# A three-block decoder on one core: the prologue in another order, the loads of units 2 and 3 held for the first row of maxima, and cross maxima among the visits in steps 6 and 7

## The chip, the cores and the metric

One core of a Trainium2 chip runs the whole program; the other seven are idle. The time is device time in microseconds of one execution, from the runtime's own clock; the profile's span, from the first to the last instruction, is a little shorter. Three runs of the kernel before are shown, and one profiled execution.

## The reference, cut to what matters

Input `x` is 8 sequences of 256 tokens with 128 features. Three residual blocks follow each other, in float32:

```
x = x + attn(layernorm(x))        # 16 heads of 8, chunks of 64 tokens; a chunk sees itself (causal) and the chunk before
x = x + xattn(layernorm(x), ctx)  # 16 heads of 8, 256 queries against 256 context tokens, with a mask and biases
x = x + ffn(layernorm(x))         # int8-rounded activations, ternary weights, 128 -> 512, a width-3 depthwise
                                  # convolution over time, silu, 512 -> 128

attn:  q, k, v = split(x @ w_qkv);  softmax(q k^T / sqrt(8) + mask) v;  @ w_out
xattn: the same with q = x Wq^T + bq, k, v from ctx;  @ Wo^T + bo
```

Each softmax subtracts its row maximum.

## The kernel before, in words

**Units and steps.** There are 16 units: units 0 to 7 are the local attention of sequences 0 to 7, units 8 to 15 the cross attention of the same sequences. The main loop (`for i in range(UNITS): iteration(i)`, one loop per engine, each an in-order instruction stream tied to the others by semaphores) runs one step per unit. Step `i` has 8 beats if it is local and 16 if it is cross (`count_of`). A beat computes one bank of scores for unit `i` on the PE, and ACT takes their exponentials into `probs` (L718). On some beats a *visit* follows (class `Local`, `Cross`, `Cross14`, `Cross15`: the beat after which each piece is issued): `qk_project` of unit `i+5` (L248 to L253), `pv`, the product of probabilities and values (L438, L451), `o_turn` (L463), `max_turn` with `v_project`, `oT_turn` with `x_turn` of unit `i+6`, and `project`, the output projection (L479).

**Maxima.** The scores of a unit are computed twice. The first time, up to two steps ahead, a "max unit" `n` (8 per local unit, 16 per cross unit) goes to bank `3 + n % 3`, and DVE reduces it to negated row maxima (`max_take`, L935). `max_range(i, k)` says which `n` fall in beat `k` of step `i`. Max unit `n` may start only when take `n - 3` is done (`m_max`). For cross units a max unit is two matmuls in one half of the rows of the array; neighbours use different halves, so a pair is issued interleaved (L303). When all maxima of a unit are there, the PE turns them (`max_turn`, L425), ACT copies them (`m_copy`, L736) and a small DMA on ACT's queue (`row`, L817) writes them as one more row of the queries, so that the second computation of the scores comes out with the maximum subtracted. `score_open` waits for that row (`m_row`).

**The split of q and k.** float32 precision in bf16 matmuls is reached by splitting each projection into high, mid and low parts, stacked over 96 rows. For units 0 to 3 ACT takes the high part and DVE the rest; from unit 4 on ACT copies the projection (`raw_copy`) and POOL makes all parts (`high_part`, `rest_part`, `mid_part`, `low_part`). The SP queue stores the parts to DRAM (`store`, 768 KB a unit with its copies) and reads them back in the stacked layout (`load`, 3 DMAs and 768 KB for a local unit) into one of 6 slots of `QK`. Each slot needs zeros once (`query_slot`, a POOL memset, L1302) and a row of ones (`query_row`).

**Prologue.** Before step 0: the first four units are projected and split by all engines together, units 0 and 1 are loaded, the PE computes max units 0 to 7 (unit 0), turns them, then max units 8 to 13 (six of unit 1). In between lie, for unit 4 and 5, `normalise` (DVE), `x_turn`, `qk_project(4)`, and `turn_over(n)`, matmuls whose result nobody reads. POOL ends its prologue with `split(4)`, the zeros of slots 4 and 5, and `mask_r` (L1342), the attention mask as a row, that cross units need. SP runs through `store`, `load` and `query_row` in a fixed order; `load(u)` waits until all parts of `u` have landed in DRAM.

**Step 0 on POOL.** `normalise(6)`, which waits for DVE's statistics of unit 6 (`x_stats`, behind the take of max unit 14); `high_part(5)`; `keep(0, 1)`, the causal select on `probs` (L1241); rest and mid part; `keep(0, 3)`; low part; `keep(0, 5)`, `keep(0, 7)`. `pv(0, 0)`, the PE's last visit of step 0, waits for the first two of these selects (`s_kept`).

## Time and profile before

| | us |
|---|---|
| median of 3 runs (295.54 to 297.85) | 296.94 |
| the profiled execution | 288.12 |
| its span | 286.3 |
| PE busy | 256.6 (90%) |
| DVE busy | 213.2 (74%) |
| ACT busy | 201.3 (70%) |
| POOL busy | 141.5 (49%) |

The rows of the profile give start and duration on a common clock from the span's start. A row with "x8" merges eight like instructions that follow each other; the bracket behind a row is the idle time of that engine before it and what ended it. "Lnnn" is a line of the kernel, often that of a helper. "SPq" and "ACTq" rows are DMA issues: how long the queue's engine was occupied, not when the data landed. PEclk is the granted clock of the tensor engine as a share of 2.4 GHz, so 0.50 is 1.2 GHz.

### The profile page before, as it was taken

How to read it: one execution, taken by the hardware profiler on the slowest of the kernel's cores; microseconds unless marked ns; L12 is line 12 of the kernel's file. 1: busy time of each engine (PE TensorE's matmuls, PEld its weight loads, DVE VectorE, ACT ScalarE, POOL GpSimd, SP SyncE). 2: the span in 40 equal slices, each digit the busy share in tenths (PEclk: the TensorE clock that was granted, in tenths of full speed). 3: DMA queues.
4: the chain of work that ended last, by engine and by line, in shares of the span. 5: the costliest groups of instructions: out<-in, count | busy, mean ns of one | idle time of the engine just before them, and what ended most of it. 6: DMA issues, size and time to landing. Idle time of an engine off the chain costs nothing.

```text
span 286.3 us, 8864 instructions
## 1 busy us (share of the span) xinstructions
PE 256.6 (90%) x3395; PEld 161.1 (56%) x3395; DVE 213.2 (74%) x543; ACT 201.3 (70%) x394; POOL 141.5 (49%) x219
## 2 busy tenths in 40 slices
PE   5778969999999999888989898898879998999992
PEld 1554657888888766554555455445434454555541
DVE  6696845676677678899788898988942468997654
ACT  1443286768878877658788887788879956677752
POOL 6579897675965956748596800000062334331000
PEclk9579799999999999999999999999999999999998
DMA  6587664694687797679646630000000000001001
GB/s 190 144 244 222 171 208 134 191 306 130 192 265 188 158 214 136 167 160 186 146 109 126 162 62 3 1 3 3 0 1 3 2 1 0 21 18 29 21 19 47
DMA packets 34435, 31.38 MB, mean 110 GB/s; under 512 B 2725, under 2 KB 30248, under 8 KB 34265
## 3 DMA queue, kind: packets, MB, share of 16 engines
q1 hardware_dynamic: 33680, 30.38, 41.7%
q8 instruction: 27, 0.44, 0.7%
q10 hardware_dynamic: 712, 0.44, 0.5%
q14 instruction: 16, 0.12, 0.1%
HBM read 16.78 MB, written 13.63 MB: 106 GB/s over the span
## 4 chain that ended last, share of the span: by engine, by line
PE 63%; DVE 11%; ACT 7%; issue 6%; POOL 5%; DMA 3%; SPq 2%; ACTq 2%; DVEq 0%; POOLq 0%
PE ps L507 11%; PE ps L438 10%; PE ps L451 6%; DVE negm L935 5%; PE ps L311 5%; PE ps L303 4%; PE ps L368 3%; PE ps L463 3%; DMA stack_parts<-low 3%; ACT probs L718 3%; PE ps L292 3%; PE ps L479 2%; ACTq L817 2%; PE ps L266 2%; PE ps L248 2%
## 5 line engine op out<-in xcount | busy, mean ns | idle before, releaser
L935 DVE TENSOR_REDUCE negm<-ps 128x2 bf16<-128x512 f32 (+1 forms) x192 | 123.0, 691 | 35.1 <-PE ps L331 12.5
L718 ACT ACTIVATE probs<-ps 128x512 f32<-128x512 f32 x192 | 103.9, 601 | 17.8 <-PE ps L368 8.4
L507 PE MATMUL ps<-tapw,xqT 128*128 128x512 f32 x96 | 45.3, 604 | 0.0
L303 PE MATMUL ps<-QK 49*128 49x256 bf16 x256 | 36.2, 272 | 3.4 <-DVE negm L935 3.3
L311 PE MATMUL ps<-QK 50*128 50x256 bf16 x256 | 35.2, 272 | 3.4 <-ACT probs L718 3.3
L438 PE MATMUL ps<-probs,V 128*32 128x256 f32 x512 | 34.1, 385 | 4.5 <-ACT V L706 4.5
L1186 POOL TENSOR_TENSOR ve<-mv,eps 128x2 f32<-128x2 f32 x8 | 1.6, 195 | 55.1 <-DVE mv L972 55.1
L311 PEld LDWEIGHTS ps<-QK 50*128 50x128 bf16 x256 | 17.5, 94 | 19.0 <-ACT probs L718 14.7
L507 PEld LDWEIGHTS ps<-tapw,xqT 128*128 128x128 f32 x96 | 16.8, 190 | 15.4 <-issue 15.4
L368 PE MATMUL ps<-QK 98*128 98x128 bf16 x256 | 23.8, 219 | 0.5
L1241 POOL TENSOR_SCALAR_AFFINE_SELECT probs<-probs 128x512 f32<-128x512 f32 x32 | 21.1, 661 | 6.0 <-ACT probs L718 5.9
L438 PEld LDWEIGHTS ps<-probs,V 128*32 128x32 f32 x512 | 13.5, 109 | 17.2 <-ACT V L706 6.2
L779 ACT ACTIVATE high<-probs,unround 128x512 bf16<-128x512 f32 x15 | 10.8, 722 | 15.3 <-DVE probs L1017 15.3
L303 PEld LDWEIGHTS ps<-QK 49*128 49x128 bf16 x256 | 16.6, 94 | 8.2 <-DVE negm L935 5.2
L368 PEld LDWEIGHTS ps<-QK 98*128 98x128 bf16 x256 | 17.3, 97 | 4.7 <-issue 1.5
L451 PE MATMUL ps<-probs,V 128*32 128x64 f32 x1024 | 17.9, 221 | 2.0 <-POOL probs L1241 1.9
L722 ACT CAST ps<-tri_k 128x512 f32<-128x512 bf16 x30 | 17.7, 590 | 0.9
L1229 POOL TENSOR_TENSOR low<-raw,mid 128x512 bf16<-128x512 f32 x15 | 17.4, 1158 | 1.8 <-DMA stack_parts<-low 1.3
L451 PEld LDWEIGHTS ps<-probs,V 128*32 128x32 f32 x1024 | 15.2, 110 | 4.2 <-issue 3.3
L1002 DVE TENSOR_REDUCE hm<-probs 128x1 f32<-128x512 f32 x16 | 10.9, 682 | 8.2 <-ACT probs L761 8.2
L1167 POOL TENSOR_TENSOR ve<-mv,eps 128x2 f32<-128x2 f32 x16 | 3.1, 195 | 25.6 <-DVE mv L895 25.4
L745 ACT COPY oxT<-ps 128x256 f32<-128x256 f32 (+1 forms) x23 | 10.4, 453 | 5.3 <-PE ps L240 4.5
(138 smaller groups left out, 500.2 us busy)
## 6 DMA issues: line engine op xcount, KB each, us to landing
QK<-stack_parts SPq DMA_DIRECT2D x24, 384.0 KB
stack_parts<-high SPq DMA_DIRECT2D x32, 192.0 KB, 4.4
stack_parts<-mid SPq DMA_DIRECT2D x32, 128.0 KB, 3.7
QK<-stack_parts SPq DMA_DIRECT2D x16, 192.0 KB
stack_parts<-low SPq DMA_DIRECT2D x16, 128.0 KB, 4.2
CT<-in_ctx_t_dram SPq DMA_DIRECT2D x1, 1024.0 KB, 7.9
out_dram<-probs SPq DMA_DIRECT2D x16, 64.0 KB, 1.6
tapw<-in_taps_dram SPq DMA_DIRECT2D x1, 768.0 KB, 6.8
```

The costliest lines, as they stand in the source:

```text
L303: last = nc.tensor.matmul(bank(3 + n % 3)[:, t * S:(t + 1) * S], QK[r, s, 0, pr, t * P:(t + 1) * P], QK[r, s, 2, pr, :], start=(t == 0), s ...
L311: last = nc.tensor.matmul(bank((before(i) + k) % 3)[:, kt * S:(kt + 1) * S], QK[r, s, 2, pr, kt * P:(kt + 1) * P], QK[r, s, 0, pr, :], sta ...
L368: last = nc.tensor.matmul(o[:, x * P:(x + 1) * P].rearrange("p (j q) -> p j q", j=2), KT[r, s, pr, WINDOWS[c]:WINDOWS[c] + P], QT[r, s, :, ...
L438: last = nc.tensor.matmul(o[32 * r:32 * r + 32, half * S:(half + 1) * S], V[:, i % 2, PAIRS * kt + 4 * half + r, 2 * m:2 * m + 2, :], prob ...
L451: last = nc.tensor.matmul(o[32 * r:32 * r + 32, st * S + c * W:st * S + (c + 1) * W], V[:, i % 2, PAIRS * V_AT[c] + 4 * st + r, 2 * m:2 * ...
L507: last = nc.tensor.matmul(bank(UP[u % 3]), xqT[:, b % 2, t * P + k:t * P + k + P], tapw[:, k, :], start=False, stop=(k == 2), skip_group_c ...
L718: nc.scalar.activation(probs[:, k, :], bank(n % 3), ACT.Exp, scale=SCALE).then_inc(s_exp, 1)
L722: nc.scalar.copy(bank(n % 3).rearrange("p (h q) -> p h q", q=W), tri_k[:, min(c, 1), :].unsqueeze(1).to_broadcast([P, 8, W])).then_inc(s_s ...
L935: nc.vector.tensor_reduce(dst, src, AX.X, ALU.max, negate=True).then_inc(m_max, 1)
L1002: nc.vector.tensor_reduce(hm[:, p, 0:1], hid[:, u % 3, :], AX.X, ALU.max, apply_absolute_value=True).then_inc(h_steps, 1)
L1229: nc.gpsimd.tensor_tensor(half_of(low, u), raw[:, :, u % 2 * S:(u % 2 + 1) * S], half_of(mid, u), ALU.subtract).then_inc(low_done, 1)
L1241: nc.gpsimd.affine_select(out=kept, in_=kept, compare_op=ALU.is_ge, fill=0.0, base=W if k >= 2 else 0, pattern=[[0, 8], [1, W]], channel_m ...
```

## The change

The change has two halves. In the prologue: PE's order (`x_turn(4)`, `x_turn(5)`, `qk_project(4)` now come after `max_turn(0)`, in other banks; ten instead of four filler matmuls ahead of max unit 0), ACT's order with it, DVE's (`normalise(4)` behind the rests of units 2 and 3, `normalise(5)` behind take 7), POOL's (`query_slot(2)` sooner; `query_slot(5)` now in step 0 behind `normalise(6)`; `mask_r` now at the end of step 1) and SP's (`store(1, 2)` ahead of `load(0)`, `store(3, 0)` ahead of `load(1)`, and `load(2)`, `load(3)` behind a new wait for the first row of maxima). In steps 6 and 7 (`B - 2`, `B - 1`): on odd beats the max units are issued after the first part of the visit instead of right behind the scores, and step 6 has two max units a beat until its 14 are out.

```diff
--- before.py
+++ after.py
@@ -70,6 +70,8 @@
     def upto(n):
         if i == 0:
             return (0, 1, 2, 2, 2, 3, 4, 5, 6)[n]
+        if i == B - 2:
+            return min(total, 2 * n)
         return min(total, n if total <= beats else -(-total * n // beats))
 
     return range(first + upto(k), first + upto(k + 1))
@@ -403,11 +405,18 @@
                         cross_beat(i, k)
                         return
                     scores(i, k)
-                    if late_pair(i, k):
+                    if late_pair(i, k) or spread(i, k):
                         return
                     if k > 0 and late_pair(i, k - 1):
                         max_late_pair(max_range(i, k - 1)[0])
                         return
+                    maxima(i, k)
+
+                def spread(i, k):
+
+                    return i in (B - 2, B - 1) and k % 2 == 1
+
+                def maxima(i, k):
                     ms = list(max_range(i, k))
                     if len(ms) == 2 and is_cross(max_unit(ms[0])[0]):
                         for m in ms:
@@ -560,6 +569,8 @@
                             pv(i - 1, 1, bank(BX), (0,))
                         if k == at.PV_B and i >= 1:
                             pv(i - 1, 1, bank(BX), (1,) if is_cross(i - 1) else (0, 1))
+                            if spread(i, k):
+                                maxima(i, k)
                         if at is Local and k == at.QK and made is not None:
                             if i >= 2:
                                 pe.wait_ge(y_done, i - 1)
@@ -570,6 +581,8 @@
                             else:
                                 pe.wait_ge(y_done, i - 1)
                             o_turn(i - 1, bank(BY))
+                            if spread(i, k):
+                                maxima(i, k)
                         if k == at.VM and i + 1 < UNITS:
                             if i >= 1:
                                 pe.wait_ge(o_done, i)
@@ -592,12 +605,16 @@
                             if turn is not None:
                                 last = x_turn(turn, bank(BY))
                             last.then_inc(xT_ps, 1)
+                            if spread(i, k):
+                                maxima(i, k)
                         if is_cross(i) and k == at.PV_A:
                             pv(i, 0, bank(BX), (1,))
                         if at is Local and k == at.PV_A:
                             pe.wait_ge(v_sb, i + 2)
                             pe.wait_ge(mT_sb, i + 2)
                             pv(i, 0, bank(BX))
+                            if spread(i, k):
+                                maxima(i, k)
                         if k == at.Y and i >= 1:
                             pe.wait_ge(xT_sb, i + 7)
                             if i == 6:
@@ -625,26 +642,24 @@
                 x_turn(3, bank(7)).then_inc(xT_ps, 1)
                 qk_project(2, bank(3))
                 qk_project(3, bank(4))
-                x_turn(4, bank(6)).then_inc(xT_ps, 1)
                 pe.wait_ge(xT_sb, 4)
-                x_turn(5, bank(7)).then_inc(xT_ps, 1)
-                qk_project(4, bank(5))
-                pe.wait_ge(xT_sb, 6)
-                turn_over(4)
+                turn_over(10)
                 pe.wait_ge(s_pc, PC_ALL)
                 pe.wait_ge(rows_in, 32)
                 for n in range(8):
                     if n < 2:
                         pe.wait_ge(rest_done, 3 + n)
-                    if n == 2:
-                        pe.wait_ge(raw_done, 1)
                     max_unit_mms(n)
-                pe.wait_ge(xT_sb, 5)
                 max_turn(0, bank(BX, BF16))
+                x_turn(4, bank(BY)).then_inc(xT_ps, 1)
+                x_turn(5, bank(1)).then_inc(xT_ps, 1)
+                qk_project(4, bank(0))
                 for n in range(8, max_end(-1)):
                     max_unit_mms(n)
                 pe.wait_ge(s_dc, CONST_ALL)
                 pe.wait_ge(v_sb, 1)
+                pe.wait_ge(xT_sb, 6)
+                pe.wait_ge(raw_done, 1)
                 for i in range(UNITS):
                     if i == 3:
                         pe.wait_ge(wc_in, 16)
@@ -842,14 +857,14 @@
                 ox_copy(2, bank(6), S, 2 * S)
                 ox_copy(3, bank(7), S, 2 * S)
                 high_copy(2, bank(3))
+                high_copy(3, bank(4))
                 v_copy(0, bank(2))
-                ox_copy(4, bank(6), S, 2 * S)
-                high_copy(3, bank(4))
-                ox_copy(5, bank(7), S, 2 * S)
-                raw_copy(4, bank(5))
                 v_slot(1)
                 m_copy(0, bank(BX, BF16))
                 row(0)
+                ox_copy(4, bank(BY), S, 2 * S)
+                ox_copy(5, bank(1), S, 2 * S)
+                raw_copy(4, bank(0))
                 act.wait_ge(s_pc, PC_ALL)
                 for i in range(UNITS):
                     iteration(i)
@@ -1126,13 +1141,14 @@
                 link(nc.vector.memset(bias3[:], 0.0))
                 nc.vector.memset(unround[:], -ROUND)
                 link(nc.vector.memset(onesb[:], 1.0))
-                normalise(4)
-                normalise(5)
                 rest_make(2, bank(3))
                 rest_make(3, bank(4))
+                normalise(4)
                 nc.vector.memset(xqT[:, :, 0:1], 0.0)
                 nc.vector.memset(xqT[:, :, S + 1:S + 2], 0.0).then_inc(padded, 1)
                 for n in range(max_end(-1)):
+                    if n == 8:
+                        normalise(5)
                     max_take(n)
                 for i in range(UNITS):
                     iteration(i)
@@ -1275,6 +1291,8 @@
                     local = not is_cross(i)
                     if i + 6 < UNITS:
                         normalise(i + 6)
+                    if i == 0:
+                        query_slot(5)
                     if i + 5 < UNITS:
                         high_part(i + 5)
                     if local:
@@ -1290,6 +1308,9 @@
                     if local:
                         for k in (5, 7):
                             keep(i, k)
+                    if i == 1:
+                        g.wait_ge(m_in, 16)
+                        nc.gpsimd.tensor_scalar(mask_r[:], mask_i, -MASKED, MASKED, ALU.mult, ALU.add).then_inc(s_mask, 1)
                     if i == 8:
                         quantise(0)
                     if i == 9:
@@ -1327,19 +1348,16 @@
                 g.wait_ge(low_done, 1)
                 mid_part(1)
                 low_part(1)
+                query_slot(2)
                 rstd_part(4, 8)
                 rstd_part(5, 10)
-                query_slot(2)
                 mid_part(2)
                 low_part(2)
                 mid_part(3)
                 low_part(3)
                 query_slot(3)
+                query_slot(4)
                 split(4)
-                query_slot(4)
-                query_slot(5)
-                g.wait_ge(m_in, 16)
-                nc.gpsimd.tensor_scalar(mask_r[:], mask_i, -MASKED, MASKED, ALU.mult, ALU.add).then_inc(s_mask, 1)
                 for i in range(UNITS):
                     iteration(i)
                 ffn_normalise(0)
@@ -1424,18 +1442,19 @@
                 store(0, 2)
                 store(1, 0)
                 store(1, 1)
+                store(1, 2)
                 load(0)
-                store(1, 2)
+                query_row(2)
                 store(2, 0)
+                store(3, 0)
                 load(1)
-                query_row(2)
                 store(2, 1)
-                store(3, 0)
                 store(2, 2)
                 store(3, 1)
-                load(2)
                 store(3, 2)
                 query_row(3)
+                sp.wait_ge(m_row[0], 16)
+                load(2)
                 load(3)
                 query_row(4)
                 stack(4)
```

## Rows read from the trace of the kernel before

**Rows 1.** Windows: busy us (x instructions) of each engine, PEclk, DMA share, GB/s.
```profile
26.00:28.00 2.00, 0.75 (x15) 0.37 (x10) 1.86 (x4) 0.00 (x0) 1.92 (x3) 1.00 0.90 254
...
29.00:32.00 3.00, 3.00 (x24) 2.01 (x22) 2.59 (x4) 0.00 (x0) 1.98 (x2) 0.50 0.45 128
...
41.00:43.00 2.00, 0.31 (x21) 0.34 (x25) 0.58 (x1) 1.51 (x3) 1.93 (x4) 1.00 1.07 313
60.00:100.00 40.00, 39.55 (x855) 32.49 (x852) 28.27 (x61) 32.48 (x66) 30.24 (x45) 1.00 0.72 201
...
114.10:127.50 13.40, 11.12 (x219) 7.54 (x215) 12.11 (x26) 8.03 (x17) 8.10 (x12) 1.00 0.77 180
```

**Rows 2.** The chain that ended last, 31 to 43 us: start us, us, what.
```profile
31.18 3.48 POOL QK L1302 x2
...
34.75 1.89 POOL mask_r L1342
...
41.93 0.63 POOL probs L1241
```

**Rows 3.** Timeline of the PE, prologue: start us, us, engine, line, what.
```profile
16.21 1.06 PE L252 MATMUL ps<-oxT,wp 128*128 128x256 f32 x2
...
18.66 0.60 PE L253 MATMUL ps<-oxT,wp 128*128 128x256 f32 x2
...
20.61 0.60 PE L252 MATMUL ps<-oxT,wp 128*128 128x256 f32 x2
...
21.48 1.03 PE L612 MATMUL ps<-identb 128*128 128x512 bf16 x4
...
22.34 0.38 PE L327 MATMUL ps<-causal,identb 128*128 128x512 bf16 x1
...
28.01 0.27 PE L425 MATMUL ps<-identb,negm 128*16 128x128 bf16 x2 [1.26 <-DVE negm L935]
...
28.21 0.39 PE L327 MATMUL ps<-causal,identb 128*128 128x512 bf16 x1
...
32.65 0.39 PE L361 MATMUL ps<-tri_k,identb 128*128 128x512 bf16 x1
...
42.69 1.10 PE L451 MATMUL ps<-probs,V 128*32 128x64 f32 x64 [1.85 <-POOL probs L1241]
```

**Rows 4.** Timeline of ACT, its queue and DVE in the prologue.
```profile
20.81 0.37 ACT L745 COPY oxT<-ps 128x256 f32<-128x256 f32 x1 [0.44 <-PE ps L240]
...
22.98 4.88 DVE L935 TENSOR_REDUCE negm<-ps 128x4 bf16<-128x512 f32 x8 [1.55 <-PE ps L331]
...
28.32 0.36 ACT L736 COPY mT<-ps 16x256 bf16<-16x256 bf16 x1 [3.24 <-PE ps L425]
...
28.71 0.60 ACTq L817 DMA_DIRECT2D QK<-mT  x1
...
35.10 0.30 DVE L895 BATCH_NORM_AGGREGATE mv<-bnst 128x2 f32<-128x6 f32 x2
```

**Rows 5.** Timeline of the SP queue: issues of load 0 and load 2.
```profile
15.17 1.21 SPq L1395 DMA_DIRECT2D QK<-stack_parts  x2
...
29.96 1.14 SPq L1395 DMA_DIRECT2D QK<-stack_parts  x2
```

**Rows 6.** The chain again: low part of unit 1, issue to landing.
```profile
17.06 3.79 DMA stack_parts<-low
```

**Rows 7.** DMA issues of the page: count, KB each, median us to landing.
```profile
out_dram<-probs SPq DMA_DIRECT2D x16, 64.0 KB, 1.6
```

**Rows 8.** Waits from 100.5 to 127 us: us in total, times, longest.
```profile
PE ps L303 <- DVE negm L935: 2.8, 5, 0.6
```

**Rows 9.** Timeline of DVE at the end of step 7.
```profile
121.60 5.07 DVE L935 TENSOR_REDUCE negm<-ps 128x2 bf16<-128x512 f32 x8
...
127.07 0.42 DVE L951 TENSOR_TENSOR X<-ps,X 128x256 f32<-128x256 f32 x1 [0.40 <-PE ps L479]
```

**Rows 10.** Timeline of the PE at the start of step 8.
```profile
127.55 0.70 PE L248 MATMUL ps<-oxT,wp 128*128 128x256 f32 x2
```

## The prediction

> **What bounds the kernel now.** I read the windows first, to see which stretch has slack. From 60 to 100 us the PE is busy 39.55 of 40 us, so whatever the prologue loses or gains goes straight into the end. Before that there are holes: 0.75 busy of 2 us at 26 to 28, 0.31 of 2 at 41 to 43, and 29 to 32 us run at a granted clock of 0.50, half speed. In step 7, from 114.1 to 127.5, the PE is busy only 11.12 of 13.4 us and DVE 12.11 [rows 1]. Then the chain: the last wait that the prologue ends with is POOL's. Two memsets of query slots (3.48, so 1.74 each, 1.8 with the start), then `mask_r` until 36.64, then step 0's POOL work up to the select `keep(0, 3)`, whose end at 42.56 releases `pv(0, 0)` [rows 2]. The PE starts it at 42.69 after 1.85 us idle [rows 3]. Behind that point no wait of any size is left until step 6, so **the start of pv(0, 0) is the figure that the first half of the change moves**. I work it out in three links.
>
> **Link 1, first row of maxima.** Before, max unit 0 starts at 22.34, behind four fillers begun at 21.48 (0.215 each), its first take at 22.98, eight takes in 4.88, `max_turn(0)` at 28.01. Now the PE is through `qk_project(3)` at 19.26 (18.66 + 0.60) and has ten fillers: 19.26 + 2.15 = 21.4, which is 0.9 sooner [rows 3, 4]. The eight takes keep their pace (DVE sets it: 0.61 each), so `max_turn(0)` comes at 27.1. DVE has `normalise(4)` ahead of them, now beside POOL's splits; it is ready by 22.0, in time for a first take at 22.1. What could hold it up is load 0, now behind `store(1, 2)` and so 0.7 later: issued from 15.9 instead of 15.17 [rows 5]. The trace does not show when it lands. Bounds: the shortest landing on the page is 1.6 us, which gives 19.4; at worst it landed just ahead of its first use at 22.55 and now lands at 23.2, and link 1 gives -0.9 + 1.7 = +0.8 instead. I take the nearest row, the low part issued right behind load 0, which took 3.79 us: the last piece of load 0, done issuing at 17.75, is there by about 21.3 [rows 6, 7]. So -0.9.
>
> **Link 2, from there to the first scores.** Before, `max_turn(0)` is followed at 28.21 by the six max units of unit 1, and the scores of step 0 start at 32.65 [rows 3]. Now two `x_turn` and `qk_project(4)` stand between. `qk_project(4)` needs `ox_copy(4)`, which ACT does after `m_copy` and after issuing `row(0)`: 0.31 until the copy starts, 0.36 copy, 0.60 issue with some 0.1 around it, 0.37 `ox_copy`, 0.14 to the PE, so 1.9 behind the start of `max_turn` [rows 4], which hides both `x_turn`. That is 29.0. The projection takes 1.2 at full clock (twice 0.60) or 2.1 at half (twice 1.06) [rows 3]. The PE again stands still just ahead of `max_turn(0)`, and before it fell to half speed right after such a hole [rows 1]; I take 2.1, so 31.1. The six max units took 4.44, most of it at half speed; at full speed they go at the takes' pace, 6 x 0.61 = 3.7. I take 4.0, some of it slow. First scores at **35.1 instead of 32.65, +2.45**. Bounds: 29.0 + 1.2 + 3.7 = 33.9, +1.25; and 31.1 + 4.44 = 35.5, +2.9.
>
> **Link 3, from the first scores to pv(0, 0).** The PE itself came to it at 40.84 (42.69 less the 1.85), 8.2 behind the first scores, so now by 43.3 at the latest: POOL decides again. POOL's step 0 needs the statistics of unit 6, which are finished at 35.4, that is 2.75 behind the first scores [rows 4], since the take of max unit 14 comes first. Before they waited 1.25 us for `mask_r` to end. Now POOL is through with its prologue early: after `qk_project(4)` a copy of 0.7 and 3.5 of `split(4)`, about 35.5, and starts with the statistics at 35.1 + 2.75 = 37.85. From there to the end of `keep(0, 3)` it was 42.56 - 36.64 = 5.92, and the memset of slot 5, 1.80, now stands in the middle of it: 45.6 [rows 2]. pv(0, 0) starts at 45.7, **+3.0**. Taking `mask_r` and one memset (3.7) out of POOL's prologue gains only the 1.25 that was really waited, and the moved memset costs 1.80 again.
>
> **Costed at nothing.** Holding loads 2 and 3: load 2 was issued at 29.96 in any case [rows 5], since it waited for its low part; the row, issued at 27.8, has landed by then with anything from 1.6 to 2.2 us. Load 3 goes directly behind it and sooner than before; it and everything queued behind on SP (`query_row(4)`, `stack(4)`) is needed only in step 1 and later. Load 2 is needed at max unit 16, 4.7 us into step 0. If the row took 6 us longer, that would be late first. `mask_r` at the end of step 1 lies in the hole that POOL has there before the next statistics, and its reader is unit 8. ACT's `v_slot(1)`, `m_copy(0)` keep their order.
>
> **Steps 6 and 7.** The PE waits for takes 5 times, 0.6 each, 2.8 together, four of them in step 7 [rows 8]: pairs of max units stand with only one beat of scores between, and the second of the pair needs the bank of the take before. In step 6 I find no gain: the singles of beats 3 and 7 become one pair (-0.3), but beats 5 and 6 now adjoin, with a wait of 0.56, and `oT_turn` waits some 0.25 for `norm`, which is now behind two takes. In step 7 the visits go between the pairs and three of four waits go; walking the beats the PE is through 1.26 sooner. But DVE does 12.11 us of work in those 13.4 [rows 1], at 0.634 a take in a row [rows 9], and now becomes the bound: its sixteen takes, norm and statistics put the residual's end at 126.8 instead of 127.49. The next `qk_project` (127.55, right behind that residual [rows 10]) waits for exactly it. So **-0.6**. Bounds: all waits gone and kept, -2.8; the visits delay DVE's first takes more than they save, +0.4.
>
> **Sum.** +3.0 - 0.6 = +2.4. Against the profiled execution: 288.12 + 2.4 = 290.5. The median of the runs lies 8.8 above that execution; I add the same to it: 296.94 + 2.4 = **299.3**.
>
> **The rule that speaks against this.** After the hole at 26 to 28 the granted clock is 0.50 from 29 to 32; after the one at 41 to 43, with even less work in it, it stays 1.00 [rows 1]. The new wait ahead of pv(0, 0), 45.7 - 43.3 = 2.4 or more, is longer than either. The Trainium skill, "TensorE: Matmul & The Clock Gate", Part 1, says that throttled is the default state and activity releases it; by that rule the longer hole is likelier to be followed by half speed. The trace agrees in one of the two holes.
>
> **The rivals.** (a) **Half speed after the longer hole**: three microseconds at 0.50 as at 29 to 32 do 1.5 us less, with load 0 perhaps late besides: 301. For it, the rule and the first hole; against it, the second. Chance 0.22. (b) **The other side, the takes as the whole story**: in steps 6 and 7 spreading removes all 2.8 us of waits because DVE's order absorbs them (it idles 1.3 in step 7 and more in step 6), while link 2 comes at its lower bound. It decides if DVE's residual ends before 126: then +1.8 - 2.8 = -1.0, 295.9. Against it, 12.11 of 13.4. Chance 0.12. (c) **The prologue change does little**: the clock doesn't fall, links 1 and 2 give +1.25 and link 3 adds 0.55, less 0.6: 298.1; or POOL's memset hides in a wait that I have wrong, and it is 297. Chance 0.18. The forecast has 0.48.
>
> **How the numbers follow.** Lower end: prologue +1.8, steps -2.8 and a little of either chance, 296.2. Upper end: +3.4 + 0.4 + 1.5, less the part that needs all three, 301.7. Within 1% is plus or minus 2.97, about what a measurement tells from no change. The forecast lies 0.6 below that border, so a third of its 0.48, most of (a), nothing of (b) and (c) go over: 0.16 + 0.18 = 0.34 slower. Faster by over 1% needs (b) and more: 0.07. Within: 0.59.
>
> **What would show it.** `max_turn(0)` near 27.1; the projection rows of unit 4 (L252, L253) from 29.0; first L361 near 35.1; a memset L1302 between L1178 and L1212 in step 0; L451 first at 45.7 behind POOL's L1241; L303 waits on L935 about 0.6 to 1.2 in sum from step 6 to 7, DVE without idle in step 7. It is wrong if the first scores start before 33.9, if pv(0, 0) isn't released by POOL, or if the PE waits elsewhere for load 2.

## The result and the profile after

The change makes the kernel slower: the ratio of its times to those of the kernel before is **1.0186, 95% interval 1.0147 to 1.0226**. On the 296.94 us that the forecast started from, that is 302.5 us. The ratio compares the executions near each kernel's fastest; single executions of the kernel before spread from 288 to 302 us, those of the changed one from 293 to 300. The plain medians of 20 each are 294.58 and 295.63, too near each other for that spread to call: what is shown is that the changed kernel no longer has executions below 292.7, where the kernel before has six below 291. A second set of runs of the unedited changed kernel gave 1.0287 (1.0229 to 1.0345). The profiled execution of the changed kernel took 295.05 us with a span of 293.3, against 288.12 and 286.3.

The windows of the changed kernel (stretch, its length, busy us and instructions of PE, PE weight load, DVE, ACT, POOL, then PEclk, DMA share, GB/s), which answer to [rows 1]:

```profile
41.00:43.90 2.90, 0.13 (x3) 0.03 (x1) 0.70 (x1) 2.22 (x5) 2.83 (x5) 1.00 0.32 103
45.00:48.40 3.40, 3.40 (x67) 2.28 (x58) 1.20 (x2) 0.80 (x2) 1.11 (x2) 0.65 0.93 283
60.00:65.00 5.00, 4.51 (x93) 3.73 (x94) 3.65 (x8) 2.23 (x4) 2.56 (x4) 0.66 0.36 104
...
121.00:133.70 12.70, 11.19 (x218) 7.54 (x216) 12.00 (x25) 8.54 (x18) 7.99 (x12) 1.00 0.60 128
```

The hole ahead of pv(0, 0) is deeper (0.13 busy of 2.9 us), and two stretches that had a granted clock of 1.00 before now have a mean of 0.65 and 0.66, so that most of each ran at 1.2 GHz: 45 to 48.4 and 60 to 65. The PE's own rows, beside [rows 3]:

```profile
27.48 0.28 PE L434 MATMUL ps<-identb,negm 128*16 128x128 bf16 x2 [1.16 <-DVE negm L950]
...
29.25 0.70 PE L254 MATMUL ps<-oxT,wp 128*128 128x256 f32 x2 [0.82 <-ACT oxT L760]
...
30.22 0.38 PE L329 MATMUL ps<-causal,identb 128*128 128x512 bf16 x1
...
33.37 0.39 PE L363 MATMUL ps<-tri_k,identb 128*128 128x512 bf16 x1
...
43.91 1.93 PE L460 MATMUL ps<-probs,V 128*32 128x64 f32 x64 [2.77 <-POOL probs L1257]
```

`max_turn(0)` is at 27.48 (28.01 before), the projection of unit 4 at 29.25, the six max units begin at 30.22 and the first scores at 33.37 (32.65 before). pv(0, 0) comes at 43.91 instead of 42.69, behind 2.77 us of idle time, and its 64 matmuls take 1.93 us where they took 1.10. What releases it is POOL (lines of the changed kernel: L1228 is the start of `split(4)`, behind 4.53 us of idle time, L1183 the start of `normalise(6)`, L1323 the zeros of slot 5, L1257 `keep`):

```profile
31.07 0.61 POOL L1228 CAST high<-raw 128x512 bf16<-128x512 f32 x1 [4.53 <-ACT raw L712]
...
36.20 0.19 POOL L1183 TENSOR_TENSOR ve<-mv,eps 128x2 f32<-128x2 f32 x1 [1.38 <-DVE mv L910]
...
38.36 1.81 POOL L1323 MEMSET QK<- 128x2048 f32 x1
...
43.10 0.66 POOL L1257 TENSOR_SCALAR_AFFINE_SELECT probs<-probs 128x512 f32<-128x512 f32 x1
```

Then a wait that the kernel before did not have, in the PE's timeline of the changed kernel, and the same thing in its chain of waits:

```profile
60.49 0.62 PE L370 MATMUL ps<-QK 98*128 98x128 bf16 x8 [1.68 <-DMA QK<-mT]
```

```profile
54.15 6.29 DMA QK<-mT
...
80.01 4.54 DMA QK<-mT
```

The row of maxima of unit 2, 8 KB on ACT's queue, was issued at 54.15 and landed 6.29 us later. The row of unit 4, issued at 80.01, took 4.54. Ahead of the row of unit 2 stood SP's transfers (timeline of the SP queue):

```profile
30.24 1.13 SPq L1413 DMA_DIRECT2D QK<-stack_parts  x2
...
48.87 1.37 SPq L1413 DMA_DIRECT2D QK<-stack_parts  x2
...
50.91 0.43 SPq L1463 DMA_DIRECT2D CT<-in_ctx_t_dram  x1
...
52.15 1.33 SPq L1396 DMA_DIRECT2D stack_parts<-high  x2
```

Load 5 (768 KB), the context (1 MB), the cross weights (256 KB) and the high part of unit 6 were issued in the 5.3 us before; the mid and low parts of unit 6 followed the row. In the kernel before load 5 left at 53.77 and the context at 55.59, behind that row's issue at 51.45.

A table by landmarks shows where the rest went. The issue of each unit's row by ACT is a landmark that every trace has.

| | before | changed | difference, running |
|---|---|---|---|
| row of unit 1 | 37.89 | 38.61 | +0.7 |
| row of unit 2 | 51.45 | 54.15 | +2.7 |
| row of unit 3 | 62.77 | 68.80 | +6.0 |
| row of unit 6 | 96.26 | 103.15 | +6.9 |
| row of unit 8 | 121.49 | 127.13 | +5.6 |
| row of unit 10 | 147.59 | 153.01 | +5.4 |
| row of unit 15 | 209.39 | 214.81 | +5.4 |
| end of the span | 286.3 | 293.3 | +7.0 |

The prologue, its hole and the late row of unit 2 bring 6.0 us up to row 3, the steps from there to row 6 another 0.9, and steps 6 to 9 give 1.5 back. The last 1.6 us come behind row 15, in a stretch with the same instructions. There the granted clock was 0.80 to 0.86 from 215 to 225 us, behind a hole of 1.78 us that every kernel of this case has. It is no mark of the change: in the 14 traces below this stretch takes 76.9 to 77.6 us where the clock between 205 and 225 us stays at 1.00 (the kernel before and experiments 1, 4 and 10), and 78.3 to 79.8 us in the ten where it falls, experiments 2, 9, 11 and 12 on the kernel before among them.

### The profile page after: what moved, and what is told of

Read it like the earlier page. It is cut to its first block, busy times and chain, and to the rows that moved or that the text cites. A ratio compares the mean times of both kernels' runs of the same rounds, so it can differ in the third digit from the quotient of the medians.

```text
span 293.3 us, 8877 instructions
## 1 busy us (share of the span) xinstructions
PE 260.4 (89%) x3401; PEld 162.0 (55%) x3401; DVE 215.1 (73%) x543; ACT 201.4 (69%) x394; POOL 142.1 (48%) x219
## 4 chain that ended last, share of the span: by engine, by line
PE 60%; DVE 16%; ACT 8%; issue 7%; DMA 4%; POOL 3%; ACTq 2%; DVEq 0%; POOLq 0%
PE ps L447 10%; PE ps L516 9%; DVE negm L950 7%; PE ps L460 5%; PE ps L313 5%; DMA QK<-mT 4%; PE ps L305 3%; PE ps L370 3%; PE ps L472 3%; PE ps L294 3%; ACT probs L733 3%; ACTq L832 2%; PE ps L250 2%; PE ps L488 2%; PE ps L254 2%
## 5 line engine op out<-in xcount | busy, mean ns | idle before, releaser
L447 PE MATMUL ps<-probs,V 128*32 128x256 f32 x512 | 34.9, 393 | 4.5 <-ACT V L721 4.5
L1257 POOL TENSOR_SCALAR_AFFINE_SELECT probs<-probs 128x512 f32<-128x512 f32 x32 | 21.1, 661 | 7.4 <-ACT probs L733 7.2
L447 PEld LDWEIGHTS ps<-probs,V 128*32 128x32 f32 x512 | 13.6, 110 | 17.7 <-ACT V L721 6.2
L460 PE MATMUL ps<-probs,V 128*32 128x64 f32 x1024 | 19.9, 232 | 3.0 <-POOL probs L1257 2.8
L460 PEld LDWEIGHTS ps<-probs,V 128*32 128x32 f32 x1024 | 17.0, 117 | 5.0 <-issue 3.6
L1183 POOL TENSOR_TENSOR ve<-mv,eps 128x2 f32<-128x2 f32 x16 | 3.4, 210 | 27.3 <-DVE mv L910 27.2
```

The source lines that it names most:

```text
L447: last = nc.tensor.matmul(o[32 * r:32 * r + 32, half * S:(half + 1) * S], V[:, i % 2, PAIRS * kt + 4 * half + r, 2 * m:2 * m + 2, :], prob ...
L460: last = nc.tensor.matmul(o[32 * r:32 * r + 32, st * S + c * W:st * S + (c + 1) * W], V[:, i % 2, PAIRS * V_AT[c] + 4 * st + r, 2 * m:2 * ...
L1257: nc.gpsimd.affine_select(out=kept, in_=kept, compare_op=ALU.is_ge, fill=0.0, base=W if k >= 2 else 0, pattern=[[0, 8], [1, W]], channel_m ...
```

## The experiments

Times are ratios to the kernel before, run on the same chip. Positions come from one profiled execution of each. This table holds, for every kernel, the distance from the first scores to pv(0, 0), the PE's idle time ahead of it, the clock behind it, and distances between issues of rows, in us. By the numbers below, "prologue only" is experiment 1, "before, steps 6 and 7 new" is 2, "slot early" 3, "context late" 4, "slot early, context late" 5, "fillers" 6, "no hold" 7, "changed, again" 8, and the last four rows are 9 to 12.

| kernel | scores to pv | hole | clock behind | row 1 to 2 | 2 to 3 | 6 to 8 | 8 to 10 |
|---|---|---|---|---|---|---|---|
| before | 10.04 | 1.85 | 1.00 | 13.56 | 11.32 | 25.23 | 26.10 |
| changed | 10.54 | 2.77 | falls | 15.54 | 14.65 | 23.98 | 25.88 |
| changed, again | 10.54 | 2.78 | falls | 17.02 | 11.32 | 23.97 | 25.90 |
| prologue only | 10.55 | 2.78 | falls | 17.03 | 11.32 | 24.84 | 25.46 |
| no hold | 10.54 | 2.77 | 1.00 | 14.06 | 12.49 | 23.78 | 26.29 |
| context late | 10.54 | 2.77 | falls | 17.01 | 11.32 | 23.78 | 26.94 |
| fillers | 10.67 | filled | 1.00 | 14.19 | 12.74 | 23.66 | 25.90 |
| slot early | 8.81 | 1.04 | 1.00 | 12.32 | 15.66 | 23.77 | 25.89 |
| slot early, context late | 8.80 | 1.03 | 1.00 | 12.32 | 11.71 | 23.76 | 25.89 |
| before, steps 6 and 7 new | 10.46 | 1.86 | 1.00 | 13.98 | 11.31 | 23.63 | 26.16 |
| before, mask moved | 8.78 | 1.04 | 1.00 | 12.32 | 11.32 | 24.83 | 25.53 |
| before, POOL part | 10.54 | 2.77 | 1.00 | 14.06 | 11.32 | 26.93 | 25.47 |
| before, mask, steps | 9.59 | 1.82 | 1.00 | 13.11 | 11.32 | 23.64 | 26.79 |
| the same with fillers | 9.36 | filled | 1.00 | 12.89 | 11.33 | 23.75 | 26.65 |

**1. The prologue alone.** In the changed kernel:

```diff
-        if i == B - 2:
-            return min(total, 2 * n)
...
-                    return i in (B - 2, B - 1) and k % 2 == 1
+                    return False
```

> The changed kernel with steps 6 and 7 as before, so the new prologue alone. Theory A (three costs of the prologue: pv(0, 0) 1.2 us later, half speed after the hole in front of it 1.5, the row of maxima of unit 2 landing 6.3 us after its issue 3.3): the row of unit 7 is issued 6.8 us later than in the kernel before, as in the changed kernel, and nothing is won back in steps 6 and 7, so about 7 us slower than before, 2.3%, and about 1.3 us slower than the changed kernel. Theory B (the steps cost, not the prologue): the time of the kernel before within 1 us.

Ratio 1.0225 (1.0161 to 1.0289). The prologue carries the loss; theory B is out. The row of unit 7 was issued at 115.63, 7.1 later than before. No row was waited for here, though: the clock stayed low for longer (0.64 from 45 to 50 us and 0.68 from 50 to 55), so that the row of unit 2 was itself issued later, at 56.82. The 1 MB of context was then 5.6 us ahead of it and not 3.2 as in the changed kernel's first trace.

**2. Steps 6 and 7 alone**, the same lines put into the kernel before:

```diff
+        if i == B - 2:
+            return min(total, 2 * n)
...
-                    if late_pair(i, k):
+                    if late_pair(i, k) or spread(i, k):
```

> The kernel before with the new order of steps 6 and 7 alone. Theory A: from the issue of the row of unit 6 to that of unit 8 it takes 24.0 us instead of 25.2, and the time falls by 0.6 (my sum) to 1.4 us (the profile of the changed kernel), 0.2 to 0.5%. Theory B (the order of steps 6 and 7 costs): 2 us or more slower.

Ratio 1.0055 (0.9945 to 1.0165), which leaves open anything from half a per cent faster to 1.6% slower. The trace says more. From row 6 to row 8 it is 23.6 to 24.0 us in all ten traces of the table with the new order and 24.8 to 26.9 in the four with the old; from row 8 to row 10 the new order is longer: 25.9 in five of the seven traces without a late row there (26.3 and 26.9 in the other two), against 25.5 in three of the four with the old order and 26.1 in the kernel before. And a late row turns up here too, in this kernel's PE timeline and its chain:

```profile
126.42 0.28 PE L313 MATMUL ps<-QK 50*128 50x256 bf16 x1 [0.55 <-DMA QK<-mT]
```

```profile
120.44 5.93 DMA QK<-mT
```

**3. The zeros of slot 5 back in POOL's prologue.** In the changed kernel:

```diff
                     if i + 6 < UNITS:
                         normalise(i + 6)
-                    if i == 0:
-                        query_slot(5)
...
                 query_slot(4)
+                query_slot(5)
                 split(4)
```

> The changed kernel with the zeros of slot 5 back in POOL's prologue, ahead of the split of unit 4, where POOL stands idle 4.5 us. Theory A: pv(0, 0) starts 1.8 us sooner, at 42.1, the hole in front of it shrinks from 2.8 to 1.0 us and the clock stays at 1.00 behind it, so the row of unit 2 is issued at 50.8 to 51 instead of 54.15 and the whole is 3 us faster than the changed kernel, if the row of unit 2 still meets the context load. Theory B (the PE itself is the limit of step 0, because of the projection of unit 4 in front): pv(0, 0) stays at 43.5 or later.

Ratio 1.0166 (1.0094 to 1.0239). This execution was late from the start (clock 0.58 from 20 to 25 us, first scores at 39.02), so distances count, not positions. The hole fell from 2.77 to 1.04 us as theory A said, and the clock behind it stayed at 1.00. The 3 us that theory A promised did not come: what was won there went into the wait for the row of unit 2, now 2.60 us, and into a clock of 0.66 from 65 to 70 us behind it. From the PE's timeline, then the chain:

```profile
47.83 1.10 PE L460 MATMUL ps<-probs,V 128*32 128x64 f32 x64 [1.04 <-POOL probs L1257]
...
63.85 0.62 PE L370 MATMUL ps<-QK 98*128 98x128 bf16 x8 [2.60 <-DMA QK<-mT]
```

```profile
56.59 7.21 DMA QK<-mT
```

Its context load was issued at 56.09, half a microsecond ahead of that row. Over the eight traces with the changed prologue the wait for the row of unit 2 follows this distance: 2.60 us for a context issued 0.5 us ahead of the row, 1.68, 1.25 and 1.01 us for 3.2, 3.2 and 3.5 us (changed, fillers, no hold), none for 5.6 and 5.8 (prologue only, changed again), and 0.23 or none where the context comes behind the row (experiments 5 and 4).

**4. The context behind that row.** In the changed kernel:

```diff
-                sp.dma_start(CT[:], ctx_t).then_inc(c_in, 16)
-                sp.dma_start(wp[:, 4:8, :]...
-                stack(6)
+                slot_free(6)
+                for part in range(3):
+                    store(6, part)
+                sp.wait_ge(m_row[0], 32)
+                sp.dma_start(CT[:], ctx_t).then_inc(c_in, 16)
+                sp.dma_start(wp[:, 4:8, :]...
+                load(6)
```

> The changed kernel with the context load (1 MB) and the cross weights behind the stores of unit 6 and behind the landing of the row of unit 2. Theory A (the row waits behind the queue of SP's transfers): the row of unit 2, issued at 54.15 as before, lands within 3 us instead of 6.3, the PE's wait for it (1.68) goes with the half speed behind it, and the row of unit 3 is issued at 65.5 to 66 instead of 68.8: 3 us faster than the changed kernel. Theory B (the wait is the load of unit 5, or the landing is slow of itself): it still lands 5 us or more after its issue and the time does not change.

Ratio 1.019 (1.0119 to 1.026): no gain. In the profiled execution the clock fell for long behind the hole (row 1 to row 2 took 17.01 us), the PE was late and waited for no row, just as in experiment 1, so this run alone does not tell the two theories apart, and the 3 us did not come.

**5. Both edits**, 3 and 4 together.

> The changed kernel with both edits of before: the zeros of slot 5 in POOL's idle stretch of the prologue, and the context load behind the landing of the row of unit 2. Theory A: hole ahead of pv(0, 0) of 1.0 us as in the run with the first edit alone, no wait of the PE for a row (there 2.6 us), and no low clock between 45 and 75 us; 3 to 5 us faster than the changed kernel, so within 1 to 2 us of the kernel before. Theory B (rows land late whatever SP has queued): a wait for a row of 1 us or more remains.

Ratio 0.9838 (0.976 to 0.9916), with the kernel before at a median of 297.23 on that chip, where none of its executions was under 293, so that the ratio flatters. The unedited changed kernel did not run on that chip, so the 3 to 5 us against it have no time beside them; what follows is read from positions in the trace. PE timeline and chain:

```profile
43.59 1.10 PE L460 MATMUL ps<-probs,V 128*32 128x64 f32 x64 [1.03 <-POOL probs L1257]
```

```profile
52.35 4.83 DMA QK<-mT
```

Against experiment 3 only the place of the context and of the transfers tied to it differs: the row of unit 2 lands after 4.83 us instead of 7.21, and the waits for rows sum to 0.5 us instead of 2.6. With the hole small and the context out of the way, row 3 is issued at 64.06, 4.7 us sooner than in the changed kernel. Counted from row 1, so that the start of the execution is left out, row 3 comes after 24.0 us, against 26.6 to 30.2 in the seven other traces with the changed prologue and 24.9 in the kernel before. That is theory A, but for one part: the row did not land within the 3 us that experiment 4 expected of it. With load 5 issued 2.5 us ahead it still took 4.83.

**6. Fillers in the hole.** In the changed kernel:

```diff
                             pe.wait_ge(mT_sb, i + 2)
+                            if i == 0:
+                                pe.wait_ge(xT_sb, 7)
+                                turn_over(10)
                             pv(i, 0, bank(BX))
```

> The changed kernel with ten matmuls whose result nobody reads in the hole ahead of pv(0, 0) (behind the wait for the copy of unit 6's turn; 2.15 us of the 2.8). Theory A (half speed after the hole costs 1.5 to 3.5 us): the hole in front of L460 is gone or under 0.7 us, the granted clock is 1.00 from 45 to 55 us, and from the issue of the row of unit 1 to that of unit 2 it takes 14.0 us instead of 15.5 to 17.0; 1.5 to 3 us faster than the changed kernel. Theory B (the low clock has nothing to do with the hole): the clock still drops and the time is the changed kernel's.

Ratio 0.9941 (0.9871 to 1.0011) on the chip of experiment 5. The window behind the hole, which had 0.64 to 0.68 in three other traces:

```profile
45.00:50.00 5.00, 4.72 (x98) 2.82 (x99) 0.90 (x2) 2.31 (x5) 4.54 (x6) 1.00 0.93 285
50.00:55.00 5.00, 5.00 (x110) 3.81 (x110) 3.30 (x10) 3.85 (x7) 3.40 (x7) 1.00 0.51 144
```

```profile
45.00:50.00 5.00, 4.84 (x121) 3.54 (x125) 2.43 (x7) 1.78 (x3) 2.66 (x6) 0.65 0.67 192
50.00:55.00 5.00, 5.00 (x82) 3.92 (x74) 1.04 (x3) 2.15 (x4) 2.71 (x5) 0.66 0.83 214
```

The first pair is this kernel, the second the unedited changed kernel. Row 1 to row 2 is 14.19 against 17.02. It then waited for the rows of units 2 and 3 (1.25 and 0.75), so part of what the clock gave was lost again. This does not show that the fillers held the clock. Experiment 7, without fillers, reached pv(0, 0) at nearly the same time (47.42, here 47.53) and behind the unfilled hole its clock was 1.00 too. The ratio does not settle it either, since the unedited changed kernel did not run on that chip, and experiment 5, with the hole shortened, has the same median there (293.08, here 293.14).

**7. No hold.** In the changed kernel, without `sp.wait_ge(m_row[0], 16)` ahead of `load(2)`.

> The changed kernel without the wait of SP for the first row of maxima ahead of loads 2 and 3. Theory A (the hold is not where the time went): load 2 is issued up to 1.5 us sooner, first scores and pv(0, 0) as in the changed kernel, time within 1 us of it; the first row lands later than before it, perhaps with a wait of up to 1.7 us for it. Theory B (the hold costs, because it lets later transfers bunch): 3 us or more faster than the changed kernel.

Ratio 1.0213 (1.0177 to 1.0249), beside 1.0287 (1.0229 to 1.0345) for the unedited one. The loss stays without the hold, so the hold is not the main cause. Whether it costs something these runs don't settle: five of the six executions (294.42 to 295.30, the sixth 299.82) are below all six of the unedited kernel on that chip (295.68 to 298.11), and the medians differ by 2.3 us, between what theory A and theory B allow; but the unedited kernel had a median of 295.63 in its first runs. The first row was not waited for here, though load 2 was issued at 28.93, ahead of the row at 29.45. This trace has the same hole and no fall of the clock behind it:

```profile
47.42 1.10 PE L460 MATMUL ps<-probs,V 128*32 128x64 f32 x64 [2.77 <-POOL probs L1257]
```

```profile
47.00:52.00 5.00, 4.58 (x165) 3.69 (x166) 2.48 (x7) 2.04 (x4) 3.21 (x6) 1.00 0.35 92
```

**8. The changed kernel again**, unedited, in that same set.

> The changed kernel once more, unedited, beside the kernel before and the three below on one chip: the level to which they are compared. Theory A: pv(0, 0) 10.5 us behind the first scores with a hole of 2.8 us; 1.5 to 2.5% slower than the kernel before where that one's short executions occur, less where they do not. From the issue of the row of unit 6 to that of unit 8 it takes 24.0 us.

Here the late side of the prologue shows: the projection of unit 4 at half speed, first scores at 34.62, pv(0, 0) at 45.16, and the clock at 0.50 from 47 to 53 us. The distances came as expected (10.54, 2.78 and 23.97); the ratio of 1.0287 is a little above the 1.5 to 2.5% expected.

**9. The kernel before with `mask_r` at the end of step 1**, nothing else.

```diff
-                g.wait_ge(m_in, 16)
-                nc.gpsimd.tensor_scalar(mask_r[:], ...).then_inc(s_mask, 1)
                 for i in range(UNITS):
                     iteration(i)
...
+                    if i == 1:
+                        g.wait_ge(m_in, 16)
+                        nc.gpsimd.tensor_scalar(mask_r[:], ...).then_inc(s_mask, 1)
```

> The kernel before with one part of the change alone: mask_r moved from POOL's prologue to the end of step 1. Theory A (POOL's chain ends with the statistics at 35.4, not with the 1.9 us of the mask): pv(0, 0) starts 1.25 us sooner, at 41.4 to 41.5, with a hole of 0.6 to 0.8 us; 1.3 us (0.4%) faster than the kernel before. Theory B (the row of unit 2 or another wait takes its place): pv(0, 0) sooner, the row of unit 3 issued as late as before, no gain.

Ratio 0.9827 (0.9761 to 0.9892), again beside a kernel before without short executions; its own shortest, 288.65, is no shorter than the kernel before gets on other chips (287.94 to 288.38), so a gain of 1.7% is not shown. From the first scores to pv(0, 0) 8.78 us instead of 10.04, which is the 1.25 expected. It is not a clean price of the mask: the first scores were late here (35.75), and POOL stood idle 4.12 us ahead of the statistics, more than the 1.9 that the mask takes. The profiled execution shows that the first row can be waited for too:

```profile
35.75 0.38 PE L361 MATMUL ps<-tri_k,identb 128*128 128x512 bf16 x1 [1.71 <-DMA QK<-mT]
...
44.53 1.10 PE L451 MATMUL ps<-probs,V 128*32 128x64 f32 x64 [1.04 <-POOL probs L1241]
```

It took 298.02 us, and so shows what a long execution of nearly the kernel before is made of. Besides that wait, a granted clock of 0.66 from 20 to 25 us and the low clock behind row 15, the PE stood still for 1.99 us ahead of 73.87 for nothing that the profile shows ("issue"), and waited 1.97 us for the row of unit 4, with a clock of 0.66 from 85 to 90 us behind it:

```profile
73.87 0.76 PE L451 MATMUL ps<-probs,V 128*32 128x64 f32 x37 [1.99 <-issue]
...
85.48 0.62 PE L368 MATMUL ps<-QK 98*128 98x128 bf16 x8 [1.97 <-DMA QK<-mT]
```

**10. The kernel before with the POOL part of the change.** As 9, and `query_slot(5)` in step 0 behind `normalise(6)`.

> The kernel before with the POOL part of the change: mask_r at the end of step 1 and the zeros of slot 5 in step 0 behind normalise(6), and PE, ACT, DVE and SP as before. Theory A (link 3 of the prediction): pv(0, 0) 0.5 us later than before, at 43.1, behind a hole of 2.3 us; time within 0.5 us of the kernel before, or 1.5 us more where the clock falls behind the hole. Theory B (the POOL part is the whole loss): 4 us or more slower.

The medians were 295.98 and, for the kernel before, 297.23: no difference to be told. Profiled, 10.54 us from the first scores to pv(0, 0) behind a hole of 2.77: +0.50 to the kernel before, and the memset's whole 1.76 more than in experiment 9. The clock did not fall behind the hole.

**11 and 12. Toward a better kernel**: the kernel before with `mask_r` moved and the new steps 6 and 7; and the same with `turn_over(5)` ahead of `max_turn(0)` and `turn_over(4)` ahead of pv(0, 0), as in experiment 6.

> The kernel before with the two parts of the change that have shown a gain in the traces: mask_r at the end of step 1, and the new order of steps 6 and 7. Theory A (gains add): pv(0, 0) 8.7 to 8.8 us behind the first scores, 24.0 us or less from the row of unit 6 to that of unit 8; 1.25 + 0.7 = 2 us faster than the kernel before, 5 us faster than the changed kernel. Theory B (what the steps save comes back as a late row or as low clock in the last step): as the kernel before with the mask moved alone, 1 us or less to be seen.

> The kernel above with matmuls whose result nobody reads in the two holes of the prologue: five ahead of max_turn(0), four ahead of pv(0, 0). Theory A (holes bring the clock down): the granted clock stays at 1.00 from 25 to 45 us, the six max units of unit 1 take 3.2 us instead of 4.4, and it is 1 us faster than the one above. Theory B (the clock falls for another reason, or the fillers delay what they stand before at half speed): equal or up to 1 us slower.

Ratios 0.9957 (0.9887 to 1.0027) and 1.0014 (0.9948 to 1.0079): by them neither differs from the kernel before. The medians of 12 executions are 293.31 and 289.88, beside 295.84 of the kernel before on that chip, and the one with fillers stays between 288.12 and 294.69, where the kernel before spreads from 287.94 to 299.84 and the one without fillers from 285.80 to 300.98. So the fillers bring no shorter best case, and in these 12 executions the long ones are missing: none above 294.69, where the kernel without fillers has 5 of 12 and the kernel before 15 of 23. How they do it the traces don't show. The clock around `max_turn(0)` was 1.00 with fillers (0.88 in the kernel before from 25 to 30 us), but it was 1.00 without them too, and the six max units took 3.2 us in both. The first line is the kernel without fillers, the second the one with them:

```profile
25.00:30.00 5.00, 3.75 (x53) 2.36 (x52) 4.00 (x8) 1.31 (x3) 4.47 (x5) 1.00 0.82 237
25.00:30.00 5.00, 5.00 (x59) 2.78 (x58) 4.08 (x8) 0.36 (x1) 3.14 (x5) 1.00 0.76 217
```

The distance from the first scores to pv(0, 0) was 9.59 us without fillers, for the 8.7 to 8.8 expected: POOL had waited 1.68 us in its prologue for the store of an earlier low part, and so came to the statistics late even without the mask. What steps 6 and 7 save is lost in good part to a late row in both (1.42 and 0.75). In the PE timeline of the kernel without fillers:

```profile
127.01 0.28 PE L313 MATMUL ps<-QK 50*128 50x256 bf16 x1 [1.42 <-DMA QK<-mT]
```

## Why the prediction was right in sign and short in size

I had forecast +2.4 us (0.8%) with an upper end of 301.7, and 0.34 for slower by over 1%. The ratio puts the result at +1.9%, 302.5 us and just past that end; by plain medians it is +0.4%. The sign was right and the likeliest case too mild. That the number is not further off is partly luck: the prologue's own delay was put 1.8 us too high against the profiled execution (+3.0 for +1.2), and that stood in for part of two costs that the sum did not have, a lower clock and a late row.

- **Link 1** held: `max_turn(0)` 27.48, and 27.3 in four other traces, for 27.1; in the remaining three with the changed prologue it came at 28.75 to 30.88, with a clock of 0.58 to 0.84 from 20 to 25 us, which the sum did not foresee.
- **Link 2** failed by its own sign in the profiled execution. I had called the forecast wrong if the first scores start before 33.9; they came at 33.37. The projection of unit 4 started at 29.25 for 29.0, but it ran at full clock where I took half, and the six max units took 3.15 us, less than the 3.7 that my lower bound gave them at the takes' pace of 0.61. With a lower clock there (experiments 1, 4, 5, 8) the first scores came at 34.55 to 34.79, for 35.1. From `max_turn(0)` on it was 5.9 us in the first trace and 7.3 to 8.1 in the seven others, for 8.0 in the sum.
- **Link 3** was exact: 10.54 or 10.55 us from the first scores to pv(0, 0) in six traces with the changed order on POOL, +0.50 for +0.55. The split is as the prediction had it: the moved memset costs 1.75 (8.80 without it in experiments 3 and 5), and in the kernel before the statistics were ready 1.25 ahead of the end of the mask. What the mask's removal gains depends on when the first scores come, as experiments 9 and 11 showed (8.78 and 9.59). The whole came out smaller, +1.2 (profiled) and +2.5 (again) for +3.0.
- **Steps 6 and 7** were right in mechanism, and in size as far as the traces agree: row 6 to row 10 takes 49.6 to 50.1 us in seven of the ten traces with the new order (50.4 to 50.7 in experiments 4, 11 and 12, the last two with a late row), and 50.3 with the old in experiments 1 and 9, a gain of 0.2 to 0.8 for 0.6. Against the profiled kernel before (51.3) it is 1.5, and experiment 10, with the old order, took 52.4, with 1.8 us of PE idle time for nothing that the profile shows. The PE's waits for takes fell from 2.8 us to 1.1, as forecast (0.6 to 1.2). The first line is from the waits of the changed kernel from 107 to 134 us; the second is its timeline, where the residual is the new bound and the PE waits for it:

```profile
PE ps L305 <- DVE negm L950: 1.1, 2, 0.5
...
133.61 0.70 PE L250 MATMUL ps<-oxT,wp 128*128 128x256 f32 x2 [0.52 <-DVE X L966]
```

- **The step that failed first: rival (a) had too little of the chance and too small a price.** Of six traces with a hole of 2.8 us, the clock fell behind it in four (changed, again, prologue only, context late) and stayed in two (no hold, POOL part). Of six with a hole of 1.0 to 1.9 it fell in none, and in neither of the two with fillers. What separates the four from the two is open. One thing on record is where they came: pv(0, 0) started between 43.91 and 45.16 in the four, at 40.68 and 47.42 in the two. Its price, read as row 1 to row 2 against the 14.06 of the two traces that kept their clock, is 1.5 us once and 3.0 three times. I had given it 0.22 and 1.5. The rule of the Trainium skill ("TensorE: Matmul & The Clock Gate", Part 1) that activity releases the throttle agrees with the shorter holes, behind which the clock fell in none of six traces. It does not tell apart the four and the two with 2.77 us, and no trace here shows that the fillers kept the clock, since experiment 7 kept it without them.
- **The step that failed second: "costed at nothing" for the SP queue.** I asked who needs load 3 and what lies behind it sooner, and not whom these transfers delay once they leave sooner while the PE is later. SP was 4 to 5 us ahead, the PE 2.7 behind, and so the context load moved from behind the row of unit 2 to in front of it. That made the wait of 1.68 us and, with the clock at 0.66 behind it, the 3.3 us between rows 2 and 3. Experiments 3 and 5, which differ in the place of the context, show the mechanism, and the distances listed under experiment 3 agree with it.
- The two losses stand in for each other. Where the clock falls for long behind pv(0, 0) the row is issued later, further behind the context, and has landed by the time it is wanted; where the clock holds, the PE waits for it. Row 3 is issued between 68.1 and 69.1 us in six traces with the changed prologue, whichever it was (at 72.25 in experiment 3, where everything was 4 us late from the start), and only removing both (experiment 5) brings it to 64.1. That fits that edits 3 and 4, one at a time, gave nothing that the times could tell.
- What stays open: why the kernel before spreads over 12 to 13 us between executions and the changed one over 8, and so why the changed one has lost the short executions. Parts of it are seen (the clock in the first 35 us, the clock behind row 15, late rows, holes put down to issue), in experiment 9 all of them at once, but no trace of a long execution of the unedited kernel before was taken.

## What to carry to other kernels

When a queue is let run ahead, list the small transfers on other queues that its large ones will now meet; here a row of 8 KB with 4.7 us of cover came onto the path when a megabyte was issued up to 3.5 us ahead of it. When work is moved out of an engine's prologue, look first for idle time where it stood: POOL had 4.5 idle us one step earlier than where the memset was put. And price a wait ahead of a PE burst with what the clock may do behind it, not only with its own length.

## What the runs showed of the hardware

- The 8 KB row on ACT's queue took 3.4 to 7.2 us to land in the traces where it was waited for, with SP's transfers under way, against 1.6 us for the 64 KB stores of the output at the end [rows 7].
- A hole of the same length ahead of pv(0, 0), 2.77 us, was followed by 3 to 4 us at a granted clock of 0.50 in one trace, by about 7 us of it in three, and by 1.00 in two; no hole of up to 1.9 us there brought the clock down. In the last step a hole of 1.78 us was followed by a fall in ten of 14 traces, so the length of a hole alone does not decide it.
- Matmuls whose result nobody reads, put into a hole of 2.8 us, cost 0.1 us of distance to pv(0, 0) (10.67 against 10.54), and the granted clock behind them was 1.00, as it was without them in experiment 7.
